# First attention: rows of maxima by DMA in place of transposes, and maximum tiles of every fourth query

## The reference

```python
x = layer_norm(x, ln_m_g, ln_m_b)            # 4 x 512 x 128
lat = layer_norm(latents, ln_l_g, ln_l_b)
q = lat @ Wq                                  # 16 heads of 64
k, v = jnp.split(jnp.concatenate([x, lat], axis=1) @ Wkv, 2, axis=-1)
dots = jnp.einsum('bhid,bhjd->bhij', q, k) * scale
attn = jax.nn.softmax(dots, axis=-1)
out = jnp.einsum('bhij,bhjd->bhid', attn, v)
```

## Time and profile before

| | |
|---|---|
| median of 3 runs | 781.49 us (780.24 to 784.04) |
| profiled execution, span from first to last instruction | 788.3 us |
| PE busy | 706.3 us (90%) |
| PEld busy | 430.8 us (55%) |
| DVE busy | 475.7 us (60%) |
| ACT busy | 378.0 us (48%) |
| POOL busy | 377.4 us (48%) |
| mean granted TensorE clock | 0.948 of full speed |
| DMA | 50.62 MB in 109867 packets |

### The profile page before, as it was taken

How to read it: one execution, slowest core, us unless ns; L and a number is a source line. 1 busy time by engine, 2 the same in 40 slices (tenths; PEclk the granted TensorE clock), 3 DMA queues, 4 the chain that set the end, 5 groups by cost and what they waited for, 6 DMA issues and landing times.

```text
span 788.3 us, 13872 instructions
## 1 busy us (share of the span) xinstructions
PE 706.3 (90%) x4810; PEld 430.8 (55%) x4810; DVE 475.7 (60%) x966; ACT 378.0 (48%) x580; POOL 377.4 (48%) x361
## 2 busy tenths in 40 slices
PE   4899999999999999999999999997995687568991
PEld 3654555545556555556545545566995343336661
DVE  4745484585585875667477478465443386845553
ACT  4475554564654554655445444344552643223440
POOL 7264453473464475444464553634333304674552
PEclk9999999999999999999999999998998697569996
DMA  9999999990000000000030004301212500122325
GB/s 253 197 201 197 204 190 10 4 4 1 1 1 2 1 14 1 1 1 1 1 121 2 1 1 108 114 24 32 72 32 80 155 1 28 35 75 69 88 66 177
DMA packets 109867, 50.62 MB, mean 64 GB/s; under 512 B 44804, under 2 KB 103048, under 8 KB 109800
## 3 DMA queue, kind: packets, MB, share of 16 engines
q1 hardware_dynamic: 106280, 42.46, 36.0%
q0 software_dynamic: 3520, 7.27, 2.7%
HBM read 20.07 MB, written 29.64 MB: 63 GB/s over the span
## 4 chain that ended last, share of the span: by engine, by line
PE 74%; DVE 11%; issue 5%; ACT 3%; POOL 3%; DMA 2%; another core or an unknown queue 1%; SPq 1%; DVEq 0%; POOLq 0%; ACTq 0%
PE PSUM L1631 14%; PE PSUM L1663 13%; PE PSUM L1598 5%; PE PSUM L1463 5%; PE PSUM L1498 4%; PE PSUM L1468 4%; PE PSUM L1729 4%; PE PSUM L1423 3%; PE PSUM L1425 2%; PE PSUM L1424 2%; PE PSUM L1612 2%; PE PSUM L1605 2%; PE PSUM L1649 2%; PE PSUM L1693 2%; DVE REC L1377 1%
## 5 line engine op out<-in xcount | busy, mean ns | idle before, releaser
L866 ACT ACTIVATE PT<-PSUM 128x1024 f32<-128x1024 f32 x128 | 128.6, 1024 | 134.1 <-PE PSUM L1631 133.7
L690 POOL TENSOR_TENSOR PSUMS<-PT 128x1024 f32<-128x1024 f32 x32 | 76.0, 2376 | 210.4 <-ACT PT L866 171.4
L690 POOL TENSOR_TENSOR PSUMS<-PSUMS,PT 128x1024 f32<-128x1024 f32 x62 | 149.6, 2413 | 16.8 <-ACT PT L866 9.9
L1254 DVE TENSOR_REDUCE TOPS<-PSUM 128x2 f32<-128x1024 f32 x128 | 152.1, 1220 | 6.9 <-PE PSUM L1598 6.5
L1663 PE MATMUL PSUM<-PT,BIG 128*64 128x512 f32 x512 | 130.6, 611 | 0.0
L1209 DVE TENSOR_TENSOR SIL<-SIL,PSUM 128x256 f32<-128x256 f32 (+1 forms) x62 | 32.2, 519 | 65.7 <-ACT SIL L783 46.8
L1244 DVE TENSOR_TENSOR KL<-PSUM,KH 128x512 fp32r<-128x512 f32 x32 | 22.1, 691 | 68.2 <-ACT KH L844 67.7
L1598 PE MATMUL PSUM<-KH,QH 64*128 64x512 f32 x256 | 57.9, 449 | 4.0 <-DVE QL L1247 3.7
L1663 PEld LDWEIGHTS PSUM<-PT,BIG 128*64 128x64 f32 x512 | 28.4, 135 | 53.4 <-issue 52.0
L1598 PEld LDWEIGHTS PSUM<-KH,QH 64*128 64x128 f32 x256 | 24.2, 183 | 59.2 <-DVE TOPS L1254 24.9
L783 ACT ACTIVATE SIL<-PSUM 128x256 f32<-128x256 f32 (+1 forms) x62 | 28.6, 462 | 56.7 <-PE PSUM L1463 31.4
(11 more groups left out here) (256 smaller groups left out, 1365.5 us busy)
## 6 DMA issues: line engine op xcount, KB each, us to landing
lists_d<-EMPTY SPq DMA_DIRECT2D x3, 2730.0 KB, 35.3
lists_b<-EMPTY SPq DMA_DIRECT2D x3, 2470.0 KB, 33.4
lists_d<-EMPTY SPq DMA_DIRECT2D x1, 2665.0 KB, 34.9
XG<-lists_d SPq DMA_DIRECT2D x39, 65.0 KB
lists_b<-EMPTY SPq DMA_DIRECT2D x1, 2405.0 KB, 17.2
BIG<-in_L_ffn_w SPq DMA_DIRECT2D x1, 2048.0 KB
W2ALL<-in_L_ffn_w SPq DMA_DIRECT2D x4, 512.0 KB, 6.2
PT<-results_d SPq DMA_DIRECT2D x8, 256.0 KB, 4.4
```

Of the source, the lines that this page charges most:

```text
L690: pool.tensor_tensor(PSUMS[:, i % 2], PTT[:, i % 2, 0] if kt == 1 else PSUMS[:, i % 2], PTT[:, i % 2, kt], ALU.add).then_inc(s_ps, 1)
L866: act.activation(PTT[:, i % 2, kt], PSUM[:, place:place + 2, :], ACT.Exp, scale=DH ** -0.5).then_inc(s_exp, 1)
L1254: dve.tensor_reduce(TOPS[:, c, 0, :], PSUM[:, place:place + 2, :], AX.X, ALU.max).then_inc(s_max, 1)
```

## The change

The four transposes and the copy go. ScalarE, at `max_turn`, waits for VectorE's joined maxima and for the context scores that last read the row buffer's slot, and issues two DMAs, one per head, from the new tile `TOP8` to the row of that head in `TOPROW`. Each takes four floats (16 bytes) from each of 128 partitions and writes 2 KB into one partition. For the four floats of a partition to be neighbours in the row, partition p has to hold queries 4p to 4p+3; so the `top` tile c now takes queries c, c+4, c+8, ..., and the weight load reads `QH` with a step of four elements. `mt` moves in `ITERATION` from behind `rows` to behind `t4`, and `max_turn` takes no PSUM banks. The joined maxima of the next pair wait until the DMAs of the last have landed. `TOPROW` is cleared once by GpSimd (128 x 2048 floats) in place of `TOPT` (128 x 192).

```diff
-        TOPT = sb("TOPT", P + 16 * TPB)
+        TOP8 = sb("TOP8", 2, TPB, dt=F32R)
...
-            "E A B PC CA0 C CA1 O0 ADD CS V qk p0 p1 t0 s0 t1 p2 t2 D s1 t3 p3 t4 P0 P2 s2 s3 rows mt O1 OUT "
+            "E A B PC CA0 C CA1 O0 ADD CS V qk p0 p1 t0 s0 t1 p2 t2 D s1 t3 p3 t4 mt P0 P2 s2 s3 rows O1 OUT "
...
-                pool.memset(TOPT[:, :], 0.0).then_inc(CONST.sem, 1)
+                pool.memset(TOPROW[:, :, :].bitcast(F32), 0.0).then_inc(CONST.sem, 1)
...
                 elif name == "max_turn":
-                    act.wait_ge(s_topt, a + 1)
+                    act.wait_ge(s_comb, a + 1)
+                    if a == 0:
+                        act.wait_ge(*CONST.at(0, "topt"))
                     if a >= GROUP:
                         act.wait_ge(s_sc, context_of(a // GROUP - 1))
-                    act.activation(TOPROW[:, a % GROUP, :], PSUM[:, place, :], ACT.Copy).then_inc(s_toprow, 1)
+                    with nc.allow_non_contiguous_dma(reason="a column of maxima becomes a row"):
+                        for h in range(2):
+                            act.dma_start(TOPROW[DH * h:DH * h + 1, a % GROUP, :].rearrange("o (q t) -> o q t", t=TPB).bitcast(F32),
+                                          TOP8[:, h, :].bitcast(F32)).then_inc(s_toprow, 16)
...
                     if a:
-                        dve.wait_ge(s_topt, a)
-                    else:
-                        dve.wait_ge(*CONST.at(0, "topt"))
-                    dve.tensor_reduce(TOPT[:, 0:P].rearrange("p (h n) -> p n h", h=2)[:, 0:16 * TPB:16, :],
-                                      TOPS[:, :, :, :].rearrange("p t a h -> p t h a"), AX.X, ALU.max).then_inc(s_comb, 1)
+                        dve.wait_ge(s_toprow, 32 * a)
+                    dve.tensor_reduce(TOP8[:, :, :], TOPS[:, :, :, :].rearrange("p t a h -> p h t a"), AX.X, ALU.max).then_inc(s_comb, 1)
...
-                            last = pe.matmul(PSUM[:, place + h, :], QH[r, i % 2, c * P:(c + 1) * P], KH[r, i % 2, :], start=True, stop=True)
+                            last = pe.matmul(PSUM[:, place + h, :], QH[r, i % 2, c:S:TPB], KH[r, i % 2, :], start=True, stop=True)
...
-                                last = pe.matmul(PSUM[:, place + h, t * M:(t + 1) * M], QH[r, i % 2, t * P:(t + 1) * P],
+                                last = pe.matmul(PSUM[:, place + h, t * M:(t + 1) * M], QH[r, i % 2, t:S:TPB],
...
-                elif name == "max_turn":
-                    pe.wait_ge(s_comb, a + 1)
-                    for t in range(TPB):
-                        last = pe.transpose(PSUM[:, place, t * P:(t + 1) * P], TOPT[:, 16 * t:16 * t + P], IDENT[:, :])
-                    last.then_inc(s_topt, 1)
-                    release(mine, (s_toprow, a + 1))
...
                         if (kt, step) == (0, 3):
-                            pe.wait_ge(s_toprow, i + 1)
+                            pe.wait_ge(s_toprow, 32 * (i + 1))
```

More of the change, by code:

```diff
@@ L271, in build @@
         s_top, s_max, s_comb = sem("top_scores"), sem("half_max"), sem("row_max")
-        s_topt, s_toprow = sem("max_turned"), sem("max_rows")
+        s_toprow = sem("max_rows")
         s_sc, s_exp = sem("scores"), sem("exps")
@@ L312, in build @@
         s_cadd = sem("c_added")
-        TAKES_BANKS = {"values", "context_values", "qk", "top", "max_turn", "scores", "context_scores", "context_sums", "spread", "out", "a_turn", "r0_turn", "r0_logits", "r0_run"}
+        TAKES_BANKS = {"values", "context_values", "qk", "top", "scores", "context_scores", "context_sums", "spread", "out", "a_turn", "r0_turn", "r0_logits", "r0_run"}
         ITERATION = (
-            "E A B PC CA0 C CA1 O0 ADD CS V qk p0 p1 t0 s0 t1 p2 t2 D s1 t3 p3 t4 P0 P2 s2 s3 rows mt O1 OUT "
+            "E A B PC CA0 C CA1 O0 ADD CS V qk p0 p1 t0 s0 t1 p2 t2 D s1 t3 p3 t4 mt P0 P2 s2 s3 rows O1 OUT "
             "O2 O3").split()
@@ L1642, in tensor_program @@
                         if step:
-                            pe.wait_ge(s_toprow, GROUP * (a + 1))
+                            pe.wait_ge(s_toprow, 32 * GROUP * (a + 1))
                         for p in range(GROUP):
```

## The result

The changed kernel took 846.54 us (median of 4 runs, 841.98 to 849.16); the kernel before, on the same chip, 782.21 us (4 runs, 780.24 to 784.04). The ratio is 1.082 (1.078 to 1.085): slower by 8%, or 64 us. The forecast was 786 us, with a range of 763 to 833. The profiled execution of the changed kernel has a span of 839.1 us, 50.8 more than the 788.3 of before.

What follows compares the result with a forecast made beforehand. TensorE, busy for 159.3 of 162 us, was taken as the bound. Transposes -16.3, strided weight loads +18.9 and late rows +2 gave +4.6 us on a 788.3 us span; less the 6.8 us offset, 786 us, range 763 to 833.

Steps and rivals of the forecast that it cites:

- the likeliest case: The forecast itself: weight loads cost about double, rows arrive in time; +4.6 us, 786 us, chance 0.38.
- Landing, "I take 2 us": Rows of maxima before the scores' fourth step: 4.7 us of room, late only during clearing; 2 us, ends 0 and 18.
- The last rival: ScalarE's DMA issue held up behind SyncE's clearing until 143 us: 833 us; issue or landing late, chance 0.13.
- The transposes, "32 x 0.51 = 16.3 us off the path": TensorE, first attention: dropping four transposes lets queries and keys start 0.51 us earlier in each of 32 pairs.
- the copy of 0.60 us that is gone pays it back: ScalarE: issuing delays the exps by about 0.47 us; the dropped copy makes this up before the queries' copy.
- It just fits: 0: Issues, exps, query and key copies and VectorE's leg take 11.1 us against a pair of 11.6: no cost.
- The ring through these copies: Issue 0.86, exps 1.96, query and key copies 1.09, VectorE to the next combining maximum 7.16: 11.1 us per pair.
- Weight loads with a step of four, +18.9 us: TensorE: 104 ns per load, exposed in the context tile and tiles 0 and 2; 0.59 us per pair.
- two ends that no row bore on: Time of a strided weight load: 55 ns at the lower end, 152 ns at the upper; the middle, 104, was taken.
- Step free: Rival on TensorE's weight loads: they keep 55 ns despite the step of four; 767 us, chance 0.34.
- step dear: Rival on TensorE's weight loads: 152 ns or worse each; 809 us, or 833 at 200 ns; chance 0.15.
- The constants on GpSimd: Clearing 2048 columns takes 1.8 us more, but MINUS is ready about 13.7 us and read at 15.42: hidden.

Runs made afterwards that it cites:

- e2: The changed kernel with contiguous weight loads, so each query gets another query's maximum subtracted: 812.48 us, ratio 1.037 to the kernel before.
- e3: The changed kernel with the clearing and numbering of the lists cut into pieces, each issued once an earlier pair's rows are there: 801.69 us, ratio 1.025.
- e1: The kernel before, transposes kept, with maximum tiles taking every fourth query and ScalarE's copy putting the row in order: 806.18 us, ratio 1.029.
- e5: e3 with ScalarE issuing the two DMAs behind the exps of the last two key tiles: 792.48 us, ratio 1.012 to the kernel before.
- e6: e5 with contiguous weight loads, subtracting other queries' maxima: 768.07 us, ratio 0.981 to the kernel before.
- e8: The changed kernel, step of four kept, clearing paced, with SyncE instead of ScalarE issuing the rows between the pieces: 793.34 us, ratio 1.014.
- e9: e8 with contiguous weight loads, subtracting other queries' maxima: 769.46 us, ratio 0.983 to the kernel before.
- e11: The kernel before, transposes kept, with weight loads of a step of two floats and ScalarE's copy in matching order: 781.62 us, ratio 0.999.
- e12: e8 with a step of two floats and four row DMAs per pair in place of two: 772.47 us, ratio 0.989 to the kernel before.
- e4: The kernel before with clearing and numbering in the same paced pieces as e3, paced by ScalarE's copies of the rows: 780.42 us, ratio 0.997.
- e10: e8 plus a ScalarE copy of the queries in tile order, so that weight loads are contiguous: 785.65 us, ratio 1.006 to the kernel before.

## Why the prediction was wrong

The sign was right for the likeliest case, the size was not: +4.6 us forecast, +64 measured. Three terms, in the order of their weight: some 40, 16 and 4 us of the 60 that were not forecast.

1. **Landing, "I take 2 us".** This step failed. With nothing late it would have been 0, its upper end was 18; pacing shows about 42. The reading of the earlier trace rows was the fault: 6.3 us was taken as a worst case, since it was one transfer behind others of its own queue. The rows come from another queue and still landed at a median of 8.5 and up to 11.4 us, against the 4.7 us of room. The price was also set as the wait alone, where a late pair does more harm: TensorE's waits on the rows are 22.5 us in six times before the scores and 5.6 us once before the context scores (view of its waits in the changed kernel, 20 to 250 us: us in total, times, longest), and the granted clock of the stretch falls to 0.92, which the prediction did not price at all. The clearing also lasts a little longer (SyncE's issues of it 40.29 and 59.26 us, in place of 36.86 and 56.70), so that 12 steps from pair to pair fall into it and not 11.

```profile
PE PSUM L1645 <- DMA TOPROW<-TOP: 5.6, 1, 5.6
```

The last rival named this place with another mechanism: ScalarE's issue held up. The issue took 0.48 to 0.88 us all through, also while SyncE's own took 16.41, so that mechanism is ruled out; the DMAs were issued in time and landed late. That its 833 us is the nearest of the forecasts to the measured time is luck.

2. **The transposes, "32 x 0.51 = 16.3 us off the path".** In the change they gave nothing in a plain pair and at most 0.2 us in the mean pair (e2 against before, e3 against e1). The step that failed is ScalarE's side, "the copy of 0.60 us that is gone pays it back" and "It just fits: 0". Two issues take 1.13 us, not 0.86. The copy that is gone stood behind the exps, the issues stand ahead of them, so it pays nothing back to whoever waits for an exp; I named the copies of queries and keys as the waiting work and missed the product of probabilities and values, which waits 0.34 us and starts 0.40 late. The ring through these copies, which was added up as 11.1 us, lacked the step's own cost in VectorE's leg; with the rows of after it is 1.13 + 1.94 + 1.09 + 7.16 + 0.71 = 12.0 us, more than the 11.6 that it should have fitted into, but less than the pair of 12.30, and tile 0 follows the product at once, 1.87 us after its start as before (316.83 to 318.70; 145.32 to 147.18). So that ring is not what ended the pair; the one through maximum, issues, exps and product is, as e5 and the longer issue in e2 show. Removing the issues from that place brought 0.38 us per plain pair in e5, e6, e8 and e9. The size was off by 0.10 as well: the projection starts 0.33 us behind the scores and not 0.23, so 0.41 us was there to gain, 13 us in all.

3. **Weight loads with a step of four, +18.9 us.** Right in mechanism, places and nearly in size: 114 ns per load against the 104 taken, tiles 1 and 3 hidden as forecast, 23 to 24 us in three comparisons (e1, e5 to e6, e8 to e9); beside late rows it is 34 (the change to e2). That 104 was near is in part luck: it was the middle of two ends that no row bore on. "Step free" is ruled out for four floats, and "step dear" too. The rule in the Trainium skill (SBUF — State Buffer, section "Door 1: The DMA port swizzle"), two hits in a line of 16 bytes for full bandwidth, is borne out on both sides: one hit doubles the load, two hits (e11, e12) leave it at 0.47 us for eight (e12's row) against 0.44. What the same section adds, that fp32 can be stepped for free by 4, is not borne out: a step of four floats doubles the load.

**The rest.** The constants on GpSimd moved the first maximum by 0.4 us, as good as hidden. The terms add up as far as they can be checked: 780.4 (e4) + 23 (step) - 0 to 6 (transposes behind a busy ScalarE) = 797 to 803 for the paced change, measured 801.7.

**Open.** The profiled executions differ by 51 us and the medians by 64. Most of that gap of 13 us is scatter: the profiled execution of the changed kernel is the fastest of its four runs (841.98 us against 846.54), and in that of the kernel before all that follows the last joined maximum took 295.9 us, where it took 284.7 to 291.0 in the twelve others (a part that no edit touches). That the lower clock of the clearing stretch follows from TensorE's standing fits the rows, clock 1.00 in e3 where nothing waits, but e3 removes the waits and the lower clock together. That a small transfer lands late because its packets share the 16 DMA engines with those of the clearing is the reading that the DMA share of 1.42 (0.38 in e3) suggests; no run isolates it. e12 stays 3 to 4 us above e6 and e9 in the medians; its mean pair is 0.02 to 0.03 us longer, which gives 1 us, and the rest is within the intervals.

## What to carry to other kernels

- A small DMA in place of on-chip work puts its landing on the path. Ask what else moves data at that moment, in any queue, and take the loaded landing (here 8.5 us against 2.0), not the quiet one; if bulk traffic with no deadline is the cause, issue it in pieces that wait for the small transfer.
- An issue holds up what stands behind it in its engine's list (here 1.13 us for two). Put it behind the work whose reader is next, or on an engine that has nothing to do, and look for every reader behind that work, not only the one on the ring that was added up.
- A layout that suits one writer can be dear for a reader that runs 256 times. Before a step of four floats, try two.

## What the hardware showed that was not expected

- A weight load of 128 columns of 4 bytes: 55 ns contiguous, 59 ns with a step of 8 bytes, 114 ns with a step of 16.
- ScalarE's copy of 128x512 floats: 595 ns contiguous, 638 ns written with a step of 8 bytes (e11), 1103 ns written (e1) and 1148 ns read (e10) with a step of 16.
- A transfer of 2 KB from ScalarE's queue beside the clearing: its issue unchanged at 0.5 to 0.6 us, its landing 8.5 us in place of 2.0. In the same stretch SyncE's own next transfer took 16.41 us to issue, while ScalarE's longest issue was 0.88: the backlog held up the issuer that made it and not the other one.
- TensorE's steps of the same kind start 0.23 us apart; the first one after a change of kind (scores to projection, scores to transposes, projection to values product) starts 0.33 us behind.
